# Edge stage of a graph network on one Trainium2 core: 54 of 391 chunks sorted by source block and summed with one-hots in place of gathers

## What is computed

```python
h = relu(_ln(x @ W1 + b1, g1, bt1))
h_src = h[src]
ef = concatenate([h_src, h[dst]], axis=1)
w = sigmoid(relu(ef @ We1 + be1) @ We2 + be2)[:, 0]      # one weight for each edge
aggr = segment_sum(w[:, None] * h_src, dst, num_segments=6250)
gate = sigmoid(concatenate([h, aggr], axis=-1) @ Wg + bg)
h_new = gate * aggr + (1.0 - gate) * h
```

## Time and profile before

| | |
|---|---|
| median of three timed runs | 2894.1 us (2892.28 to 2894.29) |
| the profiled execution, its own time | 2870.59 us |
| its span, first to last instruction | 2868.8 us |
| busy in the span: PE, DVE, ACT, POOL | 1345.9, 1615.9, 250.4, 1607.7 us |
| gathers, at L554 | 1564 |
| one-hots of the edge stage, at L1199 | 196, the first at 526.5, the last at 2753.8 us |

### The profile page before, as it was taken

The page is one execution under the profiler, slowest core; times in us unless marked ns, Lnnn a source line. Parts: engine busy times, 40 slices in busy tenths (PEclk is TensorE's granted clock), DMA queues, the critical chain, the costliest instruction groups (busy, mean ns, idle before and its releaser), DMA issues.

```text
span 2868.8 us, 34084 instructions
## 1 busy us (share of the span) xinstructions
PE 1345.9 (47%) x9754; PEld 1213.0 (42%) x9755; DVE 1615.9 (56%) x6972; ACT 250.4 (9%) x706; POOL 1607.7 (56%) x1678
## 2 busy tenths in 40 slices
PE   6999889243333333434333334343333343433361
PEld 4777677143333333333333333333333333333340
DVE  6667676355555555555555555555555555555557
ACT  1221156000000000000000000000000000000014
POOL 2000023566666666666666666666666666666656
PEclk9999968555555555555555555555555555555565
DMA  8889903444344343444444434444444344444311
GB/s 292 302 304 357 324 8 118 152 125 125 120 119 120 120 120 116 125 124 121 120 119 120 120 117 123 125 120 120 120 120 120 117 120 128 120 119 121 109 43 45
DMA packets 223573, 398.40 MB, mean 139 GB/s; under 512 B 87535, under 2 KB 108432, under 8 KB 223255
## 3 DMA queue, kind: packets, MB, share of 16 engines
q0 software_dynamic: 75072, 205.10, 24.8%
q1 hardware_dynamic: 144175, 183.08, 18.8%
q10 hardware_dynamic: 4136, 8.03, 0.8%
HBM read 381.18 MB, written 14.87 MB: 138 GB/s over the span
## 4 chain that ended last, share of the span: by engine, by line
DVE 39%; issue 37%; PE 15%; DVEq 5%; another core or an unknown queue 1%; POOL 1%; ACT 1%; ACTq 1%; DMA 0%; SPq 0%; POOLq 0%
DVE bank L327 15%; DVE weighted L333 10%; DVE bank L323 8%; PE bank L291 7%; DVEq L1228 2%; PE bank L298 2%; PE bank L880 2%; DVE sums L342 2%; DVEq L1210 2%; DVE onehot_t L1199 1%; PE bank L852 1%; PE bank L831 1%; DVEq L342 1%; PE bank L889 1%
## 5 line engine op out<-in xcount | busy, mean ns | idle before, releaser
L554 POOL DMA_INDIRECT x_rows<-src_table,lane_src x940 | 889.6, 946 | 488.7 <-issue 268.4
L318 PE MATMUL bank<-ring,onehot_t 120*128 120x128 bf16 x1564 | 197.7, 306 | 1401.7 <-issue 1345.4
L554 POOL DMA_INDIRECT ring<-src_table,lane_src x624 | 590.3, 946 | 302.2 <-issue 178.5
L318 PEld LDWEIGHTS bank<-ring,onehot_t 120*128 120x128 bf16 x1564 | 151.4, 137 | 1425.1 <-issue 1392.9
L327 DVE SCALAR_TENSOR_TENSOR bank<-bank,we_all 128x128 f32<-128x128 f32 x1564 | 413.0, 320 | 382.7 <-issue 374.8
L342 DVE TENSOR_TENSOR sums<-sums,bank 128x128 f32 (+1 forms) x782 | 189.0, 242 | 594.7 <-issue 542.4
L338 PE MATMUL bank<-weighted,x_rows 128*128 128x40 f32 x1880 | 420.6, 412 | 0.0
L338 PEld LDWEIGHTS bank<-weighted,x_rows 128*128 128x128 f32 x1880 | 415.2, 333 | 0.2 <-DVE weighted L333 0.2
L333 DVE TENSOR_SCALAR weighted<-bank,lane_dst,weight 128x40 f32<-128x40 f32 x1564 | 371.2, 308 | 1.2 <-ACT weight L755 1.2
L327 DVE DVE_READ_ACCUMULATOR bank<-bank,we_all 128x1 f32 x1564 | 203.7, 130 | 163.5 <-issue 161.5
L338 PE MATMUL bank<-weighted,ring 128*128 128x40 f32 x1248 | 279.2, 412 | 1.0 <-DVE weighted L333 1.0
(11 more groups left out here) (134 smaller groups left out, 982.1 us busy)
## 6 DMA issues: line engine op xcount, KB each, us to landing
ring<-in_edge_attr SPq DMA_DIRECT2D x195, 512.0 KB, 5.5
ring<-rel_table SPq DMA_DIRECT2D x97, 512.0 KB
x_rows<-src_table,lane_src POOLq DMA_INDIRECT x940
ring<-dst_table SPq DMA_DIRECT2D x391, 32.0 KB
ring<-src_table,lane_src POOLq DMA_INDIRECT x624
src_table<-ring SPq DMA_DIRECT2D x12, 512.0 KB, 3.7
dst_table<-ring SPq DMA_DIRECT2D x12, 384.0 KB, 2.6
h_cols<-in_x_t ACTq DMA_DIRECT2D x1, 3125.0 KB, 14.2
```

The source lines that it names most:

```text
L318: last = eng.matmul(out[:, j, :], hot_t[:, j, :], win, start=True, stop=True, skip_group_check=True)
L554: eng.indirect_dma_start(gathered(c)[:, j, :], None, src_table, bass.IndirectOffsetOnAxis(ap=lane_src[:, t:t + 1], axis=0)).then_inc(gathe ...
```

## The change

Chunks 0 to 53 are taken out of the steps, which now begin at chunk 54: 337 chunks in 169 steps, with 1348 gathers. The 216 tiles (`tokens`) of 128 edges of the first 54 chunks are handled beside these steps:

1. **Ranking**, steps 0 to 12. For each of the 49 blocks of source nodes, five at a time, every edge gets its place among the edges of its block: a compare (`in_bucket`), a running sum along each partition, and two small matmuls for the partitions before it. Each block has room for 6 cells of 128 edges.
2. **Sorting**, steps 13 to 48. For each of 216 tiles a one-hot of the row and one of the cell column times the value, and two matmuls, accumulated in PSUM over all tiles, put source-in-block and destination into the grid of cells.
3. **Out and back**, steps 50 to 59: the grid is turned, copied to bf16, written to a table in HBM and read back by broadcast, with each block's 128 rows of `src_table`, which are loaded whole.
4. **Riders**, 98 half blocks of three cells on 98 of the steps 60 to 166: one-hots of the sources and destinations make the hidden rows by matmul; dots and sigmoid give the weights; two more one-hots and a matmul build a matrix of source by destination weights (`pair_weight`); once for each block, a matmul with the block's rows of h adds to the first 128 columns of `aggr`.

Beside that, `weigh` reads its iota from SBUF and no longer from PSUM (bank 7 is needed), the 40-column sums have two banks and no longer three, the gathers of a chunk count on two semaphores and no longer four, and many `need(name, k)` are written as the `wait_ge` that they stand for. The core of the diff:

```diff
+SORTED = 54
+CAP = 6
+HALF = CAP // 2
+PART = 5
+SORT_STEP = 6
...
+    n_gather = n_chunks - SORTED
+    n_steps = -(-n_gather // 2)
+    tokens = SORTED * J
+    cells = n_blocks * CAP
+    n_parts = -(-n_blocks // PART)
+    n_riders = 2 * n_blocks
...
+        RANKED = n_parts + 2
+        SORT_AT = RANKED + 1
+        SORT_END = SORT_AT + -(-tokens // SORT_STEP)
+        CELLS_AT = SORT_END + 1
+        CELLS_OUT = CELLS_AT + 2
+        RIDE_AT = CELLS_OUT + 8
+        def ride(u):
+            return RIDE_AT + u * (n_steps - 3 - RIDE_AT) // (n_riders - 1)
+        riders = {ride(u): u for u in range(n_riders)}
+        assert len(riders) == n_riders
+        folded = {ride(2 * b + 1) + 2: b for b in range(n_blocks)}
...
-                last = eng.tensor_scalar(out[:, j, :], iota1_p, dst[:, j:j + 1], wt[:, j:j + 1], ALU.is_equal, ALU.mult)
+                last = eng.tensor_scalar(out[:, j, :], iota1[:, 0:W], dst[:, j:j + 1], wt[:, j:j + 1], ALU.is_equal, ALU.mult)
...
-            return bank[3 + c // 2 % 3][:, c % 2 * W0:c % 2 * W0 + W]
+            return bank[3 + i // 2 % 2][:, i % 2 * W0:i % 2 * W0 + W]
...
+            def block_load(b):
+                if b == 0:
+                    loaded(eng, "cell_table", 2)
+                if b >= W_SLOTS:
+                    need(eng, "hot_t", ride(2 * (b - W_SLOTS) + 1))
+                if b >= B_SLOTS:
+                    need(eng, "wsum", ride(2 * (b - B_SLOTS) + 1) + 2)
+                eng.dma_start(block_rows[:, b % B_SLOTS, :], src_table[b * P:(b + 1) * P, :]).then_inc(block_in[b % B_SLOTS], 16)
+                eng.dma_start(cell_wide[b % W_SLOTS], cell_table[:, b * CAP * P:(b + 1) * CAP * P].partition_broadcast(P)).then_inc(block_in[b % B_SLOTS], 16)
+            block_loads = {ride(2 * b) + 1: b for b in range(n_blocks)}
...
+            eng.iota(seq_i[:, 0:cells], pattern=[[1, cells]], base=-(cells // 2), channel_multiplier=0)
+            eng.iota(seq_i[:, cells:cells + 1], pattern=[[0, 1]], base=1, channel_multiplier=1)
+            eng.affine_select(out=tri, in_=ones[:, :], compare_op=ALU.is_gt, fill=0.0, base=0,
+                              pattern=[[1, P]], channel_multiplier=-1).then_inc(done("sort_iota"), 1)
...
+            for c in range(n_gather):
                 if c % 2 == 0:
                     need(eng, "wsum", c // 2 - G_SLOTS // 2)
                 if c == own_slots:
-                    need(eng, "part2", n_groups - 1)
+                    eng.wait_ge(done("part2"), n_groups)
...
+                    eng.activation(cell_weight[:, q % 4, :], cell_logit[:, q % 4, :], ACT.Sigmoid, bias=be2_all[:, 0:1])
...
+            def sort_mm(q):
+                for k, t in enumerate(sort_tokens(q)):
+                    for v in range(2):
+                        eng.matmul(cell_bank(v)[:, 0:cells], row_hot[:, q % 2, k, :], col_hot[q % 2][:, k, v, :],
+                                   start=(t == 0), stop=(t == tokens - 1), skip_group_check=True)
...
+                for k in range(HALF):
+                    o = cell_hidden(u)[:, k, :]
+                    eng.matmul(o, src_hot[:, u % 2, k * P:(k + 1) * P], block_rows[:, b % B_SLOTS, 0:P], start=True, stop=False, skip_group_check=True)
+                    for s in range(PARTS):
+                        eng.matmul(o, dst_hot[:, u % 2, k * P:(k + 1) * P], first_dst[:, s, :], start=False, stop=(s == PARTS - 1), skip_group_check=True)
...
-                need(eng, "acc2", q - 3)
+                need(eng, "acc2", q - 2)
+                if q in riders:
+                    u = riders[q]
+                    for k in range(HALF):
+                        eng.matmul(weight_out(q), place_src[:, u % 2, k, :], place_dst[:, u % 2, k, :], start=(k == 0), stop=(k == HALF - 1), skip_group_check=True)
+                if q in folded:
+                    b = folded[q]
+                    eng.matmul(folded_out(q), block_rows[:, b % B_SLOTS, P:2 * P], pair_weight[:, b % 2, :], start=True, stop=True, skip_group_check=True)
...
+            def rank_first(i):
+                bs = part_blocks(i)
+                n = len(bs)
+                eng.tensor_tensor(in_bucket[:, i % 2, 0:n, :], bucket.unsqueeze(1).to_broadcast([P, n, tokens]),
+                                  iota_b[:, bs[0]:bs[-1] + 1].unsqueeze(2).to_broadcast([P, n, tokens]), ALU.is_equal)
+                eng.drain()
+                for k in range(n):
+                    one = in_bucket[:, i % 2, k, :]
+                    eng.tensor_tensor_scan(running[:, i % 2, k, :], one, one, 0.0, ALU.add, ALU.max)
+                eng.drain()
+                eng.tensor_copy(total[:, bs[0]:bs[-1] + 1], running[:, i % 2, 0:n, tokens - 1])
+            def rank_last(i):
+                bs = part_blocks(i)
+                n = len(bs)
+                o = cell_bank(i)
+                eng.tensor_tensor(before[:, i % 2, 0:n], o[:, 0:n], base[:, bs[0]:bs[-1] + 1], ALU.add)
+                eng.tensor_reduce(fullest[:, i:i + 1], o[:, PART:PART + n], AX.X, ALU.max)
+                eng.drain()
+                for k in range(n):
+                    eng.scalar_tensor_tensor(running[:, i % 2, k, :], running[:, i % 2, k, :], before[:, i % 2, k:k + 1],
+                                             in_bucket[:, i % 2, k, :], ALU.add, ALU.mult)
+                eng.drain()
+                eng.tensor_reduce(some_pos if i else pos, running[:, i % 2, 0:n, :].rearrange("p b t -> p t b"), AX.X, ALU.add)
+                eng.drain()
+                if i:
+                    eng.tensor_tensor(pos, pos, some_pos, ALU.add)
+                    eng.drain()
...
+            def sort_hots(q):
+                for k, t in enumerate(sort_tokens(q)):
+                    eng.tensor_scalar(row_hot[:, q % 2, k, :], iota_r, row_of[:, t:t + 1], None, ALU.is_equal)
+                    for v, value in enumerate((src_low, sorted_dst)):
+                        eng.tensor_scalar(col_hot[q % 2][:, k, v, :], iota_q, col_of[:, t:t + 1], value[:, t:t + 1], ALU.is_equal, ALU.mult)
...
+            def cell_hots(u):
+                b, h = u // 2, u % 2
+                eng.wait_ge(*block_loaded(b))
+                half_ = slice(h * HALF * P, (h + 1) * HALF * P)
+                eng.tensor_scalar(src_hot[:, u % 2, :], cell_wide[b % W_SLOTS][:, 0, half_], iota_col[:, 0:1], None, ALU.is_equal)
+                eng.tensor_scalar(dst_hot[:, u % 2, :], cell_wide[b % W_SLOTS][:, 1, half_], iota_col[:, 0:1], None, ALU.is_equal)
...
+                if q == 0:
+                    sort_start()
+                if 0 <= q - 2 < n_parts:
+                    rank_last(q - 2)
+                if q < n_parts:
+                    rank_first(q)
+                elif q == RANKED:
+                    ranked()
+                elif SORT_AT <= q < SORT_END:
+                    if q == SORT_AT:
+                        for i in range(min(SRC_SLOTS, n_groups)):
+                            loaded(eng, f"src_table{i}", slot_uses(i, SRC_SLOTS))
+                    sort_hots(q)
+                elif q == CELLS_AT:
+                    cells_in()
+                elif q == CELLS_OUT:
+                    cells_turned()
+                elif q in riders:
+                    cell_hots(riders[q])
...
+            def cell_weigh(u, q):
+                for k in range(HALF):
+                    at = u * HALF + k
+                    eng.tensor_scalar(place_src[:, u % 2, k, :], iota_s, cell[:, 0, at:at + 1], None, ALU.is_equal)
+                    eng.tensor_scalar(place_dst[:, u % 2, k, :], iota_s, cell[:, 1, at:at + 1], cell_weight[:, q % 4, k:k + 1], ALU.is_equal, ALU.mult)
...
+                if q in riders:
+                    need(eng, "weight", q - 4)
+                    edge_dots(eng, cell_logit[:, q % 4, :], cell_hidden(riders[q]), HALF)
...
+                if q in riders:
+                    b, h = riders[q] // 2, riders[q] % 2
+                    if h == 0:
+                        eng.tensor_copy(pair_weight[:, b % 2, :], weight_out(q))
+                    else:
+                        eng.tensor_tensor(pair_weight[:, b % 2, :], pair_weight[:, b % 2, :], weight_out(q), ALU.add)
+                if q in folded:
+                    eng.drain()
+                    eng.tensor_tensor(aggr[:, 0:P], aggr[:, 0:P], folded_out(q), ALU.add)
```

More of the change, by code:

```diff
@@ L417, in _ @@
                 if s == min(V_SLOTS, n_supers - 1):
-                    need(eng, "rel", 0)
+                    eng.wait_ge(done("rel"), 1)
                     for g in range(row_groups):
@@ L545, in _ @@
                 loaded(eng, f"src_table{k}", slot_uses(k, SRC_SLOTS))
-            need(eng, "res", n_groups - 1)
-            for c in range(n_chunks):
+            eng.wait_ge(done("res"), n_groups)
+            for c in range(n_gather):
                 if c % 2 == 0:
@@ L1250, in far @@
                 eng.wait_ge(done("far_acc2"), item + 1)
-            need(eng, "acc2", n_pairs - 1)
+            eng.wait_ge(done("acc2"), n_steps)
```

(2 more changed lines are left out.)

291 lines of the change are left out of this document (229 added, 62 removed).

## The result

| | before | after |
|---|---|---|
| median of four timed runs | 2893.32 us | 2699.89 us (2693.93 to 2707.43) |
| profiled execution, its span | 2870.59, 2868.8 us | 2697.62, 2695.9 us |
| gathers; one-hots of the edge stage | 1564; 196 | 1348; 169 |
| first and last one-hot | 526.5, 2753.8 us | 542.2, 2575.1 us |

The ratio is 0.9333 (95% interval 0.9308 to 0.9358). 2734 us were predicted, with a range of 2540 to 3060.

The account below looks back on a forecast made before the run. The gather stream was taken to set the pace, 11.48 us a step. The edge stage falls from 2250 to 2072 us (-178), +18 for the start: 2870.6 becomes 2711, plus 23.5 to the median, 2734 us; range 2540 to 3060.

Parts of the forecast that it names:

- The removed 27 steps: Edge stage: 196 steps become 169, and 27 steps of 11.48 us save 310 us.
- VectorE's own 11.2 us plus a pause: Sorting steps: upper bound of 11.2 + 2.96 = 14.2 us a step, with 11.48 below; 12.3 was taken.
- The start: Before the edge steps: small instructions 3 us, `sort_start` 5 and a delayed first `wsum` 10, together +18 us.
- The reading of the second half of a cycle: Every second edge step: gathers set the pace, VectorE and TensorE get little done, one 2.96 us pause per two steps.
- the lower end for riders: Rider steps: at least today's 11.48 us, 10.0 of gather issue and 1.48 of pause.
- The upper end: Rider steps: a pause after each step instead of each second, 10.0 + 2.96 = 12.96 us; the middle, 12.2, was taken.
- Late cells: Rider steps: SP runs only one or two steps ahead; a late transfer would stop `cell_hots` and VectorE's queue; expected covered.
- Full cover: Rival for the edge stage: idle time takes all new work, steps except ranking stay at 11.48 us; 2626 us, chance 0.18.
- Nothing is hidden: Rival for the edge stage: each added us of VectorE work is paid, 566 us in all; 3168 us, slower, chance 0.18.
- The pause goes: Rival for the edge stage: VectorE's load dissolves the 16-gather cycle into the gathers' 10.0 us a step; 2437 us, chance 0.10.
- The port: Rival: each SBUF compare beside gathers is held 0.24 us by the port VectorE shares with GpSimd; 3025 us, chance 0.08.
- It doesn't do its work: Rival: an overfull block or too large a destination makes further windows do the 54 chunks one by one; chance 0.01.

Follow-up runs that it names:

- the two experiments: Changed kernel without all work on the first 54 chunks, ratio 0.8937; and without only riders, their block loads and folds, 0.9104; each against the kernel before.
- the gathers spaced: Kernel before with a memset of 128 columns on GpSimd behind each gather from the seventh chunk on, two semaphores for a chunk's gathers: ratio 1.0002.
- the last run: Changed kernel with three blocks ranked in a step, six slots for a block's rows and a 1000-column GpSimd memset behind each eighth gather: 0.9101, 2616.29 us.
- before_sbuf_iota: Kernel before with one edit, the weighing compare reading its iota from SBUF instead of PSUM: ratio 0.9997.
- the long rest: Kernel before with a memset of 2000 columns on GpSimd behind each eighth gather, two semaphores for a chunk's gathers: ratio 1.0107.
- the short rest: Kernel before with a memset of 1000 columns on GpSimd behind each eighth gather, run twice: 1.0616 (2742.31 us) and 1.0655 (2755.75 us).
- Half the gathers: Kernel before with only two of each chunk's four gathers issued: ratio 0.6571, 1886.65 us.

## Why the prediction came out nearly right

**The removed 27 steps.** 310 us forecast, 305 measured alone.

**What is paid for the added work.** Forecast 150 us: 2072 - 169 x 11.48 = 132, and 18 for the start. Measured 114 by the ratios. The spans of the profiled executions differ by 138; the kernel before took 22 us more beside the change (2893) than on the chip of the two experiments (2871), which is most of the 24 between. The shares: ranking, sorting and start 80 forecast and 48 measured; riders 98 x 0.72 = 71 and 66. By part, forecast and profile: ranking steps 14.5 and 14.94 us, the three behind them 12 and 10.3, sorting 12.3 and 11.74, riders with their plain steps 12.1 and 12.08.

These lengths look closer than the reasons were. I took 11.48 us as what every step costs without the new work, and in the first ten it is 9.65. So ranking costs 51 us where 10 x (14.5 - 11.48) = 30 were forecast, and sorting 3 where 36 x 0.82 = 30 were. For sorting I went between the cycle and VectorE's own 11.2 us plus a pause, and it ran at the cycle's pace with VectorE busy for 10.2 us. The two misses offset each other, which is luck.

**Durations.** The sizes of 128 and 294 columns held (261 and 374 ns with the overlap counted in, against 270 and 390), riders cost 290 us over 98, 2.96 and not 3.2. In ranking the miss is `tensor_reduce` over 1080 elements with a stride: 2.27 us, not 1.2. The scans are 586 ns long and 0.52 us apart (25.6 us for 49), where 0.45 was taken and 0.55 the upper bound. By such rows a whole ranking step adds about 9.0 us to VectorE, without the drains, and not 7.6.

**The start.** +18 forecast. The first one-hot is 15.7 us later, and the tail, put at nothing, is 5.9 us longer.

**From profile to median.** I added the 23.5 us by which the medians of before lay above its profiled execution. That execution (2870.59 us) lies 22 us below the fastest of the runs timed beside the change (2892.28) and is what three other chips give (medians of 2871.23, 2872.25 and 2872.70), so it may be of another chip; the record doesn't say. The changed kernel's profiled execution is one of its four timed runs, 2.3 us below their median. By the medians the kernel moved by 193 us against 160 forecast, and this difference of 33 is in the main the added work, 114 for 150; by the profiled executions it moved by 173, of which a part would then be the chips'.

**The reading of the second half of a cycle.** The point the forecast said it hung on was half right. Right: the gathers set the pace, and VectorE is held up by them without being busy (6.36 us a step when half of them go). Not right: that one pause belongs to each unbroken run of 16. With the gathers spaced the pause came mostly every 24 and the time stayed, and in the last run GpSimd still waited behind most of its rests. What stays in the kernel before is the mean of about 1.435 us a gather on these chips. It gives the lower end for riders, 8 x 1.435 = 11.48, by another road. The upper end, 12.96, had a pause of 2.96 us over the gap behind each 8 gathers; GpSimd's 104 waits with a releaser unknown are 2.2 us on the mean, and the steps with riders run at 1.50 us a gather. Nothing on record derives that figure, so my middle of 12.2 hit the measured 12.08 partly by luck. Late cells are a part of the extra that the forecast named as a danger and put at nothing: 29 us of waits in the group of L1486.

**Rivals.** *Full cover* falls by the riders (66 us paid) and holds for sorting. *Nothing is hidden* falls (21% are paid). *The pause goes* isn't seen on the chips of the change's own measurement, but on two others its 10.0 us a step is what the kernel before must have by its time, and the changed kernel with `PART = 3` and six slots has 1.258 us a gather there. The change as it is wasn't run on such a chip, nor was the kernel before profiled there. *The port* falls: L1516 has 481 ns on the mean, L1199 had 488; gathers take 959 ns for 946, and within a run they are issued 1.258 us apart on the mean for 1.251, 10 us over all 1348. The Trainium skill, page "SBUF — State Buffer", section "Who interferes with whom", has two-port VectorE instructions and GpSimd exclude each other; beside gathers of this size the runs show no price for that over the 0.1% of `before_sbuf_iota` and, for the compares of ranking, sorting and riders, over those 10 us. *It doesn't do its work* falls too: GpSimd issued 1348 gathers and none more, so the loop of `further_windows` was never entered.

## What to carry to other kernels

A periodic pause is not yet a cause: space the work, rest, and add slots, and see whether the pause or the mean rate is what stays. Idle time of an engine beside a saturated gather stream did take four fifths of 541 us of new work here, so work that removes gathers may be large, as long as each step's share stays under the stream's own step and is spread evenly. Read what a step costs without the new work at the place where the new work goes: the first ten steps here take 9.7 us and the others 11.5. Take the kernel before anew on every chip, its profile too, and don't carry an offset between profiled and timed executions over to the changed kernel.

## What the hardware showed unexpectedly

- In four of the six sets of timed runs the gather stream of 128 rows of 1 KB costs the kernel before about 1.435 us each at the mean, though one is issued in 1.25 us, and VectorE stands in the middle of its work while it is made up; TensorE waits for VectorE's logits, by the `need(eng, "logit", q - 2)` of its `hidden_mm`. SyncE is slowed as well: with the long rest 117 of its 542 instructions between 800 and 1750 us took over 0.5 us, with the short rest, on a chip without blocking, 11 of 570. In the two other sets, each on a chip of its own, the stream costs nothing more: 2582 and 2586 us for the same kernel instead of 2871 to 2893.
- The cause stays open. It isn't the DMA engines' share (0.41, and 0.56 where nothing was blocked), and it isn't a backlog of transfers: by the packets of the gathers' queue in the kernel before, the 4th to the 16th gather of a run have landed 2.4 to 2.7 us after their issue (medians), the late ones no later than the early, and the first three take 3.3 to 3.8 us. Spacing, slots and the place of the iota don't move it.
- The traces of the two kinds of chip differ in one more thing, and it is the strongest rival left. Counted over the same 55 to 95% of the gathers, the kernel before has 2.9 semaphore events a microsecond on record. The kernel with the long rest, on the chip with blocking, has 5.1, and the one with the short rest, on chips without, 16. Half the gathers: 8.1. Between 100 and 300 us, ahead of the gathers, all traces have 13.7. A gather adds 16 to its semaphore, and on the chips without blocking 15.9 to 16.0 events a gather are on record. The kernel before has 3.1 of the 16, the changed one 3.5, half the gathers 6.7 and the long rest 6.2. So most events are missing in the traces with blocking, which is why many releasers are "remote" there; in the traces without it no wait of a gather is named so. The Trainium skill, page "NOTIFIC — Programmer's Manual", section "When the ring fills", lists losing records and stalling the producer as two of three answers of a full record queue. Whether the recording itself stalls the engines on these chips was not tested: all executions here were recorded.
- TensorE's granted clock rose with its load: 0.50 and 0.51, the lower level of 1.2 GHz, in ranking and plain steps, 0.60 while sorting and 0.63 with riders, between that and 2.4 GHz. A matmul of `wsum` takes 332 ns on the mean and not 412, so the riders' matmuls were partly paid by a faster clock. The forecast counted them all at the lower level.
